# A two-layer attention network on one NeuronCore: one issue-order table replaced by another

## The reference

```python
# layer 0
h = x + attention(rms(x), rms(x), sa_wq, sa_wk, sa_wv, sa_wo)          # rms: rmsnorm with its own weight
h = h + attention(rms(h), context, ca_wq, ca_wk, ca_wv, ca_wo)
h = h + (silu(rms(h) @ w_gate) * (rms(h) @ w_up)) @ w_down
# layer 1
norm_X = layernorm(context);  norm_F = layernorm(h)
attended = softmax(norm_F @ norm_X.T * D ** -0.5) @ norm_X
hid   = gelu(attended @ fc1_w.T + fc1_b)                                # 4 columns
cross = hid @ fc2_w.T + fc2_b
nc    = layernorm(cross)
self_ = softmax(nc @ nc.T * D ** -0.5) @ nc
out   = norm_F + gamma2 * (cross + gamma1 * self_)
```

## Time and profile before

| | |
|---|---|
| median of 3 runs | 982.89 us (982.67 to 984.75) |
| profiled execution | 982.89 us, span 981.0 us |
| TensorE matmuls | busy 879.7 us, 90% (weight loads 737.0 us, 75%) |
| VectorE | 659.7 us, 67% |
| ScalarE | 545.0 us, 56% |
| GpSimd | 256.7 us, 26% |
| memory read and written | 22.85 MB and 9.24 MB |

### The profile page before, as it was taken

The page is one execution under the profiler, slowest core; times in us unless marked ns, Lnnn a source line. Parts: engine busy times, 40 slices in busy tenths (PEclk is TensorE's granted clock), DMA queues, the critical chain, the costliest instruction groups (busy, mean ns, idle before and its releaser), DMA issues.

```text
span 981.0 us, 21973 instructions
## 1 busy us (share of the span) xinstructions
PE 879.7 (90%) x7962; PEld 737.0 (75%) x7962; DVE 659.7 (67%) x1417; ACT 545.0 (56%) x1096; POOL 256.7 (26%) x545
## 2 busy tenths in 40 slices
PE   3686879999999999999999999999999999989773
PEld 2665667787878788888888787878878888778762
DVE  3367475859596867778695959686777869555431
ACT  3354545465666565665746565656566574735332
POOL 6000001113141313232222214132323232323242
PEclk9679999999999999999999999999999999979785
DMA  5533332121221313131112112131313121101000
GB/s 176 193 119 105 112 104 98 43 80 61 66 86 38 114 37 116 37 110 40 64 50 96 52 64 84 36 113 36 113 36 114 38 59 52 56 15 54 4 12 22
DMA packets 74624, 71.25 MB, mean 73 GB/s; under 512 B 17632, under 2 KB 67408, under 8 KB 74560
## 3 DMA queue, kind: packets, MB, share of 16 engines
q1 hardware_dynamic: 74560, 70.39, 22.3%
HBM read 22.85 MB, written 9.24 MB: 33 GB/s over the span
## 4 chain that ended last, share of the span: by engine, by line
PE 54%; DVE 24%; issue 10%; ACT 9%; DMA 1%; POOL 1%; SPq 0%; DVEq 0%; ACTq 0%; POOLq 0%
PE mring L1209 14%; PE ring L1209 10%; DVE mx_sa L1049 9%; PE od L1316 6%; PE ring L1302 6%; PE down_ps L1349 5%; PE ring L1282 4%; ACT probs L858 3%; PE mring L1378 2%; DVE late_b L1067 1%; DVE late_a L1102 1%; DVE late_a L1096 1%; PE ring L1217 1%; DVE hT_a_lo L1023 1%; PE mring L1454 1%
## 5 line engine op out<-in xcount | busy, mean ns | idle before, releaser
L858 ACT ACTIVATE probs<-ring 128x1024 f32<-128x1024 f32 (+1 forms) x192 | 190.9, 1024 | 35.9 <-PE ring L1302 35.1
L1049 DVE TENSOR_REDUCE mx_sa<-ring 128x4 f32<-128x1024 f32 x128 | 152.9, 1212 | 9.8 <-PE ring L1282 9.8
L621 POOL TENSOR_TENSOR hidT_lo<-late_a,hidT_hi 128x256 fp32r<-128x256 f32 x128 | 94.6, 739 | 218.1 <-ACT hidT_hi L885 218.1
L875 ACT ACTIVATE late_a<-mring 128x256 f32<-128x256 f32 x128 | 48.6, 380 | 94.3 <-PE mring L1209 80.7
L1054 DVE TENSOR_REDUCE mx_ca<-ring 128x4 f32<-128x308 f32 x128 | 54.9, 471 | 66.4 <-PE ring L1282 66.2
L1102 DVE SCALAR_TENSOR_TENSOR late_a<-late_a,mring 128x256 f32<-128x256 f32 x128 | 52.7, 412 | 55.9 <-ACT late_a L875 55.9
L1282 PE MATMUL ring<-pk_sa 63*128 63x256 f32 x512 | 65.3, 336 | 21.4 <-DVE mx_sa L1049 6.8
L1349 PE MATMUL down_ps<-down_hi,hidT_hi 128*128 128x256 f32 x256 | 79.4, 310 | 0.0
L1282 PEld LDWEIGHTS ring<-pk_sa 63*128 63x128 f32 x512 | 39.4, 191 | 47.9 <-DVE mx_sa L1049 11.2
L1349 PE MATMUL down_ps<-down_lo,hidT_hi 128*128 128x256 f32 x256 | 72.1, 282 | 0.0
L1349 PE MATMUL down_ps<-down_hi,hidT_lo 128*128 128x256 f32 x256 | 72.0, 281 | 0.0
(11 more groups left out here) (276 smaller groups left out, 2266.6 us busy)
## 6 DMA issues: line engine op xcount, KB each, us to landing
pk_sa<-qkT SPq DMA_DIRECT2D x96, 256.0 KB, 2.7
qpk_ca<-qkT SPq DMA_DIRECT2D x48, 256.0 KB, 2.6
x_sb<-x SPq DMA_DIRECT2D x16, 256.0 KB, 3.2
x_res<-x SPq DMA_DIRECT2D x16, 256.0 KB, 2.9
out<-o_sb SPq DMA_DIRECT2D x16, 256.0 KB, 2.5
kpk_ca<-k_ca SPq DMA_DIRECT2D x48, 77.0 KB, 2.5
vz_ca<-v_ca SPq DMA_DIRECT2D x16, 154.0 KB
v_ca<-v_all SPq DMA_DIRECT2D x4, 512.0 KB, 3.8
```

Source lines behind the costliest of these rows:

```text
L621: nc.gpsimd.tensor_tensor(hidT[1][:, m % HID, :], hid[:, m % 2, :], hidT[0][:, m % HID, :].bitcast(F32), ALU.subtract).then_inc(S["hidlo"] ...
L858: nc.scalar.activation(granule(g, tag)[0:rows_, i0:i0 + 2, :, :].rearrange("p i h t -> p h i t"), ring_tile(("E", tag, k))[0:rows_].rearra ...
L1049: nc.vector.tensor_reduce(mx[tag][:, :, :, k].rearrange("p q h -> p h q"), ps[:].rearrange("p h (q t) -> p h q t", t=T), AX_X, ALU.max).th ...
```

## The change

The text of `ORDER` is replaced, for all five engines; nothing else differs. The set of steps is the same, each with new neighbours and in part a new number of batches ahead. The first line of TensorE's string, before and after:

```diff
     "pe": """
-        f2@-4 gu.5@-2 gk.3@0 gv.3@0 E.ca.0@-1 E.ca.1@-1 gk.1@1 gk.4@-1 gu.6@-2 gT.1@3 gu.7@-2 gv.1@1 E.ca.2@-1 E.ca.3@-1 pv.ca.0@-1 S.sa.0@1 dnp.3@-2
+        gu.5@-2 qk.sa@1 f2@-4 pv.sa.2@0 pv.sa.3@0 gT.0@3 gT.2@1 kg@1 E.ca.0@-1 E.ca.1@-1 gu.6@-2 gv.4@-1 gu.7@-2 gv.2@1 gv.3@0 E.ca.2@-1 E.ca.3@-1 pv.ca.0@-1
```

36 lines of the change are left out of this document (18 added, 18 removed).

## The result

The new order is slower: 1011.86 us median against 983.37, ratio 1.0289 with a 95% interval of 1.0243 to 1.0335, where 976 was forecast. The kernel before stayed within 982.67 to 984.75 us in this comparison, and within 980.3 to 988.3 us in all later ones. Executions of the kernel after spread from 1006 to 1018 us (nine of them, with a median of 1009.9 us), and their mean granted TensorE clock from 0.929 to 0.914, against 0.954 in the profiled execution before. The profiled execution after is the quickest of them, 1005.76 us with a span of 1004.0, so what follows divides up 23.0 us and not the 28.5 us between the medians; that the other executions after are longer goes with their lower clocks. These are its answers to the earlier trace rows: the clock in 40 slices, then stretches (length, busy time and instructions of PE, PEld, DVE, ACT, POOL, then PE's clock, DMA share, GB/s).

A forecast was written before the change was run, and what follows sets the result against it. A period was taken as bound by TensorE's work (51.51 of 53.10 us) plus 1.6 us of waits. From a 981.0 us span, head −7.5, periods +5 and tail −4.5 gave 974.0 span, 976 us; range 964 to 990.

The forecast's parts named there:

- Head, −7.5: Start of the kernel, once: earlier first q/k evacuation, packs and first scores save 7.5 us; bounds −1 and −10.
- the second batch's q/k comes another 2.5 us sooner: Head: the second half's pack no longer delays the next score steps, so the second batch's q/k gains another 2.5 us.
- less DMA time: Head, counter-effect: TensorE reaches the periods sooner, leaving less DMA time for the weights; no separate size given.
- Rival 2: Head and tail gain nothing: head +1, tail −3, period +0.2; 983 us, same as before; chance 0.16.
- Exp stretch, +1.0 a period: Shifted-score steps E0 to E7, each period: TensorE newly waits 1.0 us for ScalarE; bounds 0 and 1.4.
- TensorE's own sum of 7.3 us from E0 to E7: Exp stretch: TensorE's work from E0's start to E7's issue takes 7.3 us, against 8.3 us needed by ScalarE.
- Score stretch: Self-attention score steps, each period: old waits −1.2 us, new wait +0.8, net −0.4; bounds −1.2 and +0.8.
- the e2 wait: Score stretch, each period: e2 directly behind S4 waits for mT2's evacuation on ScalarE, +0.8 us.
- the credit of 1.2 us for the old waits: Score stretch, each period: S steps spaced further apart remove waits behind wo.ca's residual add and ahead of v.sa, −1.2 us.
- Packing, −0.2: Each period: four lone E steps become two pairs, saving TensorE 0.2 us; bounds −0.6 and 0.
- an exp stretch with one more 1 us wait keeps its clock: Exp stretch, each period: TensorE's clock stays up despite the added wait of about 1 us.
- Tail, −4.5: Last batches, once: e2 and u2 fill the wait ahead of T.mlp and the clock partly holds, −4.5 us; bounds 0 and −7.

The follow-up runs named there:

- b_head: Kernel before, with only the priced head part: first norm and q/k evacuation earlier on ScalarE, context-value store behind both packs on SyncE; 982.6 us, ratio 0.999.
- b_once_after: Kernel before, with only the steps that run once (loads, splits, context keys and values, folds) placed as in the kernel after; 1004.1 us, ratio 1.023.
- b_exp_pairs: Kernel before, with only the exp stretch of the kernel after (E steps in four pairs) on TensorE, ScalarE and VectorE; 1013.5 us, ratio 1.030.
- b_u2_ahead: Kernel before, with only u2 moved ahead of gate/up 0 on TensorE and VectorE; 995.3 us, ratio 1.010.
- b_fill: Kernel before, with idle products added ahead of the first scores and of T.mlp and gate/up 0 in the last two batches; 983.4 us, ratio 1.000.

## Why the prediction was wrong, point by point

**Head, −7.5: the sign was wrong, +10.2.** The steps up to the first scores came close to what was worked out. The first q/k product starts 3.5 us sooner, at 28.93 for 32.40, and its evacuation no longer waits behind a context product's. The first scores start at 41.56, for which 40 to 41 stood (timelines of ScalarE, SyncE's queue and TensorE, the answers to the earlier trace rows):

```profile
31.97 1.08 ACT L833 ACTIVATE qkT<-ring 128x512 fp32r<-128x512 f32 x2 [2.66 <-PE ring L1209]
```

```profile
33.97 4.01 SPq L553 DMA_DIRECT2D pk_sa<-qkT  x6
```

```profile
41.56 0.94 PE L1282 MATMUL ring<-pk_sa 63*128 63x256 f32 x8
```

The evacuation is 7.9 us sooner and not 5.6, because the product ran at a clock of 1.00 and took 3.0 us where it had taken 5.3; that part was luck. The step that failed is the one that carried this on, "the second batch's q/k comes another 2.5 us sooner", and with it −7.5 us for all that follows. The second q/k comes 1.3 us sooner, the third 6.7 us later, the fourth 10.2 us later. The rows show how, from the first to the second q/k and from the second to the third, each before and after:

```profile
39.82:75.15 35.33, 25.83 (x182) 19.66 (x184) 19.93 (x25) 16.95 (x25) 1.66 (x1) 0.76 0.43 142
31.97:73.81 41.84, 32.02 (x218) 26.06 (x220) 19.97 (x24) 17.59 (x26) 0.69 (x1) 0.71 0.38 125
```

```profile
75.15:117.36 42.21, 30.86 (x276) 24.16 (x280) 26.67 (x41) 19.46 (x34) 1.38 (x2) 0.92 0.34 110
73.81:124.03 50.22, 38.26 (x264) 29.50 (x267) 26.66 (x42) 18.72 (x32) 1.38 (x2) 0.69 0.30 98
```

In the first pair TensorE is idle as long as before (9.5 and 9.8 us) and busy 6.2 us longer: these are the 36 matmuls (124 less 88) that were put behind the first q/k, among them the fold. They fill the wait of 5.18 us for the packs, and other waits take its place. In the second pair it is busy 7.4 us longer with 12 matmuls fewer, at a clock of 0.69 for 0.92, and idle 0.6 longer. Over all three the 54 further matmuls are 5.6 us at the mean of a period, an estimate from 51.51 us for 494, and the other 12.8 us of busy time stand beside a clock of 0.79 for 0.89. The prediction looked at what stood ahead of the first q/k and gave one clause to the other side, as "less DMA time"; the moved work and the clock had no term. b_head shows the priced part at zero, b_once_after that the order of the steps that run once brings most of the longer busy time. Why the clock is lower there, and how much of the 12.8 us a higher one would give back, stays open. Rival 2 had a head that gains nothing, at +1, and not a loss.

**Exp stretch, +1.0 a period: sized too high.** The wait behind the exps is 0.16 us, on E7 as forecast (timeline of TensorE in the period from 607.40):

```profile
640.17 0.51 PE L1209 MATMUL mring<-hT_m_hi,gate_hi 128*128 128x256 f32 x2 [0.28 <-DVE late_a L1104]
647.41 0.50 PE L1302 MATMUL ring<-pk_sa 64*128 64x256 f32 x4 [0.16 <-ACT probs L858]
```

and a gate/up step waits 0.28 us for VectorE, which gets its tanh later because two exps stand ahead of it on ScalarE. Together 0.44. The term that was mis-sized is TensorE's own sum of 7.3 us from E0 to E7. E0 starts at 639.04 and E7 at 647.41, which is 8.37 us; without the 0.44 of waits TensorE needed 7.9. ScalarE's 8.3 was right, so the difference is 0.4 and not 1.0.

**Score stretch: the e2 wait was right, the rest was not.** 0.92 us were measured, 0.8 forecast, with the releaser named. But the credit of 1.2 us for the old waits was too large: 0.21, 0.22 and 0.36 us of waits stand in the stretch after, where 0.46, 0.28 and two smaller ones stood. **Packing, −0.2:** TensorE's busy time in a period at a clock of 1.00 is 51.39 against 51.51, so −0.1; in b_exp_pairs the pairs alone made it 0.6 longer. The three together: 53.74 − 53.10 = +0.6 in this period, where +0.4 was forecast. The sum of the waits was close, and over the twelve periods idle time grows by 6.4 of the 17.8 us. As single terms were off both ways, that it was close is in part luck.

**The clock in the periods: missing.** The remaining 11.5 us of the twelve periods are longer busy time with the same matmuls, from the low phases. The prediction used the trace's rule that 1.6 us of scattered waits leave the clock at 1.00, and took it that a period with 2.3 us of them would, too; so it said, with the Trainium skill's rule beside it, that "an exp stretch with one more 1 us wait keeps its clock". The exp stretch did. The score stretch did not, and no term, rival or bound had a price for that: it costs 1.2 to 2.5 us in a period that has a phase. The Trainium skill, "TensorE: Matmul & The Clock Gate", section "Why this matters for your kernels", speaks of idle gaps; here filling the one gap that stood out took the lost cycles from 17.0 to 10.2 us and did not end the phases. The fills in both places and the one move in b_u2_ahead show that here the run of small products counted beside the gap, which no row of the kernel before could show. What made it visible in advance, if anything, was the order: between wo.ca and gate/up 0 ten small steps in a row (nXT, S3, mT2, S4, e2, S5, S6, T.mlp, u2, S7), where before there were four and, behind v.sa, five.

**Tail, −4.5: −5.1, for other reasons.** The waits moved as forecast, and e2 now stands in the old one of 3.16:

```profile
893.81 0.50 PE L1446 MATMUL mring<-sidesT 128*128 128x256 f32 x2 [1.78 <-ACT sidesT L930]
895.05 0.87 PE L1217 MATMUL mring<-ident,late_a 128*128 128x128 f32 x4 [0.74 <-DVE late_a L1018]
```

But TensorE's idle time in the tail is 34.8 us where it was 35.0, so nothing was won by filling. What shrank is its busy time, 147.6 to 142.7 us. About 2 us of that are the 18 matmuls that now stand ahead of the q/k mark and are counted in the head, and cycles lost fell from 26.2 to 23.6 us. Half of the forecast was for a clock that holds behind the wait; it did not hold (0.87 in the second row is T.mlp at the falling clock). The 3.16 us were also misread: the row names nXT's evacuation, the reader that frees the tile, and not the MLP's normed input, and in b_fill the fill waits for it in T.mlp's place. The size was right by luck.

**The chances.** Slower had 0.24, by waits alone, at 989 us. Head and clock both went past the worst case. The head's bounds were −1 and −10, with nothing above zero, though the deferred matmuls could be read in the order of TensorE.

## What to carry to other kernels

Work that is moved behind a milestone is not won until it is known where it now lies: count the instructions ahead of the milestone in both orders, and follow busy and idle time to the next milestones. If the mark itself has changed places with other steps, part of a difference is only counted elsewhere. Where TensorE is busy all the time, look at the longest run of small products and waits between two large ones, not only at the waits; one exchange of neighbours cost 12 us here, about half of it through the clock. An order of one engine is repaired only together with that of the engines that serve it: four plausible repairs all came out slower. And work that is added to fill a wait must be seen in the trace to lie inside it; a fill that waits for the same tile as the step behind it comes on top.

## What the runs showed of the hardware that I had not expected

Phases of low clock in the periods, where TensorE is nearly always busy, cost most of their lost cycles: 3.4 lost made a period 2.5 us longer (53.74 to 56.22), and 17.0 lost in twelve periods stand beside 11.5 us more busy time. And in b_u2_ahead the clock fell behind a run of steps, from v.sa to u2, in which the longest wait is 0.25 us and TensorE's records leave hardly a gap; I had taken idle time to be what it needs.
